# Gate and up products of a feed-forward as three products of rounded parts, with the low-rank product on 96 rows

## The reference

```python
mod = MOD_SCALE * jnp.tanh(attn @ A)
h = _rmsnorm(residual, ln2_w)
gate_pre = h @ W_in_base.T + mod * (h @ A) @ B
gate = jax.nn.silu(gate_pre)
up = h @ W_up_base.T
mlp_out = gate * up @ W_down.T
```

## Time and profile before

| | us |
|---|---|
| median of 3 runs | 1212.7 |
| lowest and highest | 1212.69, 1216.48 |
| the profiled execution | 1211.12 |
| its span, first to last instruction | 1209.3 |
| PE busy | 1038.0 (86%), x6621 |
| VectorE busy | 722.9 (60%), x1630 |
| ScalarE busy | 523.0 (43%), x881 |
| POOL busy | 308.2 (25%), x618 |
| mean granted TensorE clock | 0.917 of full |
| share of PE in the chain that ended last | 74% (VectorE 17%, ScalarE 4%) |
| page's slice from 393 to 423 us (14 of 40) | PE busy 7 tenths, clock 7 tenths of full |

### The profile page before, as it was taken

How to read it: one execution, slowest core, us unless ns; L and a number is a source line. 1 busy time by engine, 2 the same in 40 slices (tenths; PEclk the granted TensorE clock), 3 DMA queues, 4 the chain that set the end, 5 groups by cost and what they waited for, 6 DMA issues and landing times.

```text
span 1209.3 us, 18846 instructions
## 1 busy us (share of the span) xinstructions
PE 1038.0 (86%) x6621; PEld 660.5 (55%) x6621; DVE 722.9 (60%) x1630; ACT 523.0 (43%) x881; POOL 308.2 (25%) x618
## 2 busy tenths in 40 slices
PE   6399999999999788887889899962566978999997
PEld 4378888888887333333556337342223434556575
DVE  6965544544447568767655124487796665684744
ACT  3332222222243676665545411334553644544643
POOL 3024343434435555335331200010312200000000
PEclk9589999999999789899999999995767889999999
DMA  5202111121450000000000300020000000000000
GB/s 147 54 14 51 41 45 46 41 50 39 121 161 1 1 3 3 2 2 3 2 3 4 122 1 1 0 53 0 1 2 1 3 2 1 1 10 1 9 9 10
DMA packets 62461, 32.10 MB, mean 27 GB/s; under 512 B 47121, under 2 KB 61089, under 8 KB 62129
## 3 DMA queue, kind: packets, MB, share of 16 engines
q1 hardware_dynamic: 62384, 31.10, 9.6%
HBM read 29.64 MB, written 1.05 MB: 25 GB/s over the span
## 4 chain that ended last, share of the span: by engine, by line
PE 74%; DVE 17%; ACT 4%; issue 3%; POOL 1%; DMA 1%; POOLq 0%; DVEq 0%; SPq 0%; ACTq 0%; PEldq 0%
PE bank L780 16%; PE bank L806 8%; PE bank L915 4%; PE bank L1204 3%; PE bank L1388 3%; PE bank L1030 2%; PE bank L1133 2%; PE bank L998 2%; PE bank L1405 2%; PE bank L1390 2%; PE bank L960 2%; DVE mx L2379 2%; PE bank L1184 2%; PE bank L1220 1%; PE bank L1392 1%
## 5 line engine op out<-in xcount | busy, mean ns | idle before, releaser
L2379 DVE TENSOR_REDUCE mx<-bank 128x2 f32<-128x512 f32 (+1 forms) x176 | 117.7, 689 | 74.9 <-PE bank L1133 37.9
L1799 ACT ACTIVATE prob<-bank 128x512 f32<-128x512 f32 x176 | 103.2, 599 | 84.3 <-PE bank L1184 56.2
L1567 ACT ACTIVATE hhi<-hh 128x512 fp32r<-128x512 f32 x72 | 45.6, 633 | 156.1 <-DVE hh L2215 143.0
L2211 DVE TENSOR_TENSOR hu<-bank,sg 128x512 f32<-128x512 f32 x64 | 44.3, 692 | 92.1 <-PE bank L780 92.1
L780 PE MATMUL bank<-xh,wh 128*128 128x512 f32 x288 | 91.8, 400 | 0.3 <-DVE hh L2215 0.3
L780 PE MATMUL bank<-xh,wl 128*128 128x512 f32 x288 | 90.9, 396 | 0.0
L780 PE MATMUL bank<-xlo,wh 128*128 128x512 f32 x288 | 90.6, 396 | 0.0
L2203 DVE TENSOR_TENSOR hlo<-hh,hhi 128x512 fp32r<-128x512 f32 x72 | 57.2, 794 | 50.4 <-ACT hhi L1567 50.4
L2802 POOL TENSOR_TENSOR wl<-wraw,wh 128x512 fp32r<-128x512 f32 x72 | 81.6, 1133 | 13.0 <-POOL wh L2799 13.0
L1645 ACT ACTIVATE sg<-bank 128x512 f32<-128x512 f32 x72 | 43.1, 598 | 64.0 <-PE bank L780 64.0
L2799 POOL CAST wh<-wraw 128x512 fp32r<-128x512 f32 x72 | 37.1, 515 | 102.6 <-issue 51.8
(11 more groups left out here) (466 smaller groups left out, 2223.0 us busy)
## 6 DMA issues: line engine op xcount, KB each, us to landing
wraw<-in_L_ffn_wg_dram SPq DMA_DIRECT2D x64, 64.0 KB, 2.2
wraw<-in_L_ffn_wu_dram SPq DMA_DIRECT2D x64, 64.0 KB, 2.4
wraw<-in_L_ffn_wd_dram SPq DMA_DIRECT2D x32, 128.0 KB, 2.5
l_raw<-in_L_ffn_w_dram SPq DMA_DIRECT2D x2, 1024.0 KB, 6.6
mun<-in_L_ffn_mu_dram SPq DMA_DIRECT2D x1, 2048.0 KB, 7.5
xs<-in_x_dram SPq DMA_DIRECT2D x2, 512.0 KB, 4.5
w1s<-in_L_ffn_W_dram SPq DMA_DIRECT2D x2, 512.0 KB, 8.1
stage<-in_L_ffn_W_in_base_dram SPq DMA_DIRECT2D x1, 1024.0 KB, 8.1
```

The source lines that it names most:

```text
L1567: return act.activation(dst, src, ACT.Copy, scale=scale)
L1799: act.activation(t.prob[k][:, :], bank[3 + n % 2][:, :], ACT.Exp).then_inc(S("probs"), 1)
L2211: tt(hu[k % 2][:, :], bank[4 + (n + 1) % 4][:, :], sg[k % 2][:, :], ALU.mult).then_inc(once("up_used"), 1)
L2379: V.reduce_max(out_, bank[n % 3][:, :].rearrange("p (h t) -> p h t", h=heads), AX, negate=True)\
```

## The change

Weights, inputs and the low-rank factors of the feed-forward are taken apart into a part rounded to fp32r ("high") and the rest ("low"), and each product of gate and up becomes high x high + low x high + high x low. `am`, `bm`, `wa` and `mh` get three strips of 32 rows or columns, of which the first 16 hold data; in the low-rank product the strips of B are high, high, low and those of `mh` high, low, high, so that one matmul on 96 rows makes the sum of the three. POOL rounds `winT`, `wupT` and `bm` at the end of the first attention stream; VectorE makes the low parts after the meeting; ScalarE rounds `hT` between its tanh and sigmoid work; VectorE makes `hT_low`. New tiles lie over tiles that are no longer used; `gu` keeps 9 blocks instead of 16.

```diff
-        wa = sb("wa", [P, DC, R])
-        am = sb("am", [P, DC, R])
-        bm = sb("bm", [R, F1])
+        wa = sb("wa", [P, DC, 3 * 32])
+        am = sb("am", [P, DC, 3 * 32])
+        bm = sb("bm", [3 * 32, F1])
...
-            W(am[:, :, :], I["L1_ffn_A"].rearrange("(c p) r -> p c r", p=P)).then_inc(rest, 16)
-            W(bm[:, :], I["L1_ffn_B"]).then_inc(rest, 16)
+            sp.wait_ge(once("strips_cleared"), 1)
+            for j in range(3):
+                W(am[:, :, 32 * j:32 * j + R], I["L1_ffn_A"].rearrange("(c p) r -> p c r", p=P)).then_inc(rest, 16)
+                W(bm[32 * j:32 * j + R, :], I["L1_ffn_B"]).then_inc(rest, 16)
...
-                    mm(bank[4 + h][0:R, :], am[:, cc, :], hT[:, cc, h * 512:(h + 1) * 512], start=cc == 0, stop=cc == 1)
+                    mm(bank[4 + h][0:96, :], am[:, cc, :], hT[:, cc, h * 512:(h + 1) * 512], start=cc == 0, stop=cc == 1)
...
+                if n == 0:
+                    pe.wait_ge(once("ffn_weights_rounded"), 2)
+                    pe.wait_ge(once("ffn_weights_rest"), 2)
+                if f == 0:
+                    pe.wait_ge(once("hT_rounded"), h + 1)
                 g, u = bank[2 * (n % 2)], bank[2 * (n % 2) + 1]
-                for cc in range(DC):
-                    mm(g[:, :], winT[:, cc, fs], hT[:, cc, tok], start=cc == 0, stop=False)
-                for cc in range(DC):
-                    mm(u[:, :], wupT[:, cc, fs], hT[:, cc, tok], start=cc == 0, stop=cc == 1)
+                for to, high, low in ((g, win_high, win_low), (u, wup_high, wup_low)):
+                    for j, w in enumerate((high, low, high)):
+                        if f == 0 and j == 2:
+                            pe.wait_ge(once("hT_rest"), h + 1)
+                        for cc in range(DC):
+                            x = hT_low[:, cc, tok] if j == 2 else hT_high[:, h, cc, :]
+                            mm(to[:, :], w[:, cc, fs], x, start=j == 0 and cc == 0, stop=to is u and j == 2 and cc == 1)
                 pe.wait_ge(S("mh"), h + 1)
-                mm(g[:, :], bm[:, fs], mh[:, tok], start=False, stop=True).then_inc(S("ffn_up"), 1)
+                if n == 0:
+                    pe.wait_ge(once("bm_split"), 1)
+                mm(g[:, :], bm_parts[:, fs], mh[:, tok], start=False, stop=True).then_inc(S("ffn_up"), 1)
...
-                act.activation(modT[:, h * 512:(h + 1) * 512], bank[6 + h][0:R, :], ACT.Tanh).then_inc(S("modT"), 1)
+                act.activation(modT[:, h * 512:(h + 1) * 512], bank[6 + h][0:96, :], ACT.Tanh).then_inc(S("modT"), 1)
+
+            def round_inputs(h):
+
+                act.wait_ge(S("mod_ps"), HALVES)
+                copy(hT_high[:, h, :, :], hT[:, :, h * 512:(h + 1) * 512]).then_inc(once("hT_rounded"), 1)
+
+            round_inputs(0)
             for h in range(HALVES):
                 act.wait_ge(S("c_turned"), h + 1)
                 copy(cT8[:, h * 512:(h + 1) * 512], bank[6 + h][0:CD, :]).then_inc(S("cT2"), 1)
+            round_inputs(1)
...
             dve.wait_ge(once("batch_cleared"), 2)
 
+            for n, (low, whole, high) in enumerate(((win_low, winT, win_high), (wup_low, wupT, wup_high))):
+                dve.wait_ge(once("ffn_weights_rounded"), n + 1)
+                tt(low[:, :, :], whole[:, :, :], high[:, :, :].bitcast(F32), ALU.subtract).then_inc(once("ffn_weights_rest"), 1)
+            dve.wait_ge(once("bm_rounded"), 1)
+            tt(bm_parts[64:96, :], bm[64:96, :], bm_parts[64:96, :].bitcast(F32), ALU.subtract).then_inc(once("bm_split"), 1)
...
-                stt(out=mh[:, tok], in0=modT[:, tok], scalar=0.1, in1=bank[4 + h][0:R, :], op0=ALU.mult, op1=ALU.mult)\
-                    .then_inc(S("mh"), 1)
+                step(stt(out=modT[:, tok], in0=modT[:, tok], scalar=0.1, in1=bank[4 + h][0:96, :], op0=ALU.mult, op1=ALU.mult))
+                step(V.tensor_copy(mh[:, tok], modT[:, tok]))
+                tt(mh[32:64, tok], modT[32:64, tok], mh[32:64, tok].bitcast(F32), ALU.subtract).then_inc(S("mh"), 1)
+                dve.wait_ge(once("hT_rounded"), h + 1)
+                tt(hT_low[:, :, tok], hT[:, :, tok], hT_high[:, h, :, :].bitcast(F32), ALU.subtract).then_inc(once("hT_rest"), 1)
...
+            step(G.memset(am[:, :, :], 0.0), G.memset(bm[:, :], 0.0))
+            pool.sem_inc(once("strips_cleared"), 1)
             pool.sem_inc(once("picks"), 2)
...
             attention(step, "A")
+            pool.wait_ge(S("scores"), tiles_before("A", None))
+            pool.sem_inc(once("went_on"), 1)
+            for high, whole in ((win_high, winT), (wup_high, wupT)):
+                G.tensor_copy(high[:, :, :], whole[:, :, :]).then_inc(once("ffn_weights_rounded"), 1)
+            G.tensor_copy(bm_parts[:, :], bm[:, :]).then_inc(once("bm_rounded"), 1)
             end_loop(3 + 4)
```

More of the change, by code:

```diff
@@ L249, in flamingo @@
         early = top[0]
+        at_winT = top[0]
         winT = sb("winT", [P, DC, F1])
@@ L350, in flamingo @@
         after_operands = top[0]
+        at_hT = top[0]
         hT = sb("hT", [P, DC, TOKENS])
@@ L405, in flamingo @@
         top[0] = after_hT
-        gu = sb("gu", [P, HALVES, F1 // P, 512])
+        win_high = sb("win_high", [P, DC, F1], FR)
+        gu = sb("gu", [P, F1 // P + 1, 512])
         sgf = [sb(f"sgf{k}", [P, 512]) for k in range(2)]
-        modT = sb("modT", [R, TOKENS])
-        mh = sb("mh", [R, TOKENS])
+        wup_high = sb("wup_high", [P, DC, F1], FR)
+        modT = sb("modT", [3 * 32, TOKENS])
+        mh = sb("mh", [3 * 32, TOKENS], FR)
         assert top[0] <= after_c
+        top[0] = at_winT
+        win_low = sb("win_low", [P, DC, F1], FR)
+        wup_low = sb("wup_low", [P, DC, F1], FR)
+        top[0] = at_wqkvT
+        bm_parts = sb("bm_parts", [3 * 32, F1], FR)
+        top[0] = at_hT
+        hT_low = sb("hT_low", [P, DC, TOKENS], FR)
         top[0] = after_c
@@ L432, in flamingo @@
         mu2 = sb("mu2", [P, DC, SLOTS])
+        at_atT = top[0]
         atT = sb("atT", [P, DC, TOKENS])
+        top[0] = at_atT
+        hT_high = sb("hT_high", [P, HALVES, DC, 512], FR)
         top[0] = after_c
@@ L525, in prep_bank @@
             return ((6, 7, 3) if g < 12 else (4, 5, 3))[g % 3]
-        REST = len(rowsD) - 2 + 8
+        REST = len(rowsD) - 2 + 12
         def clear(eng, spared=()):
@@ L872, in _ @@
                 for cc in range(DC):
-                    last = mm(bank[7][:, m * R:(m + 1) * R], wo[:, cc, m * P:(m + 1) * P], am[:, cc, :],
+                    last = mm(bank[7][:, m * 96:(m + 1) * 96], wo[:, cc, m * P:(m + 1) * P], am[:, cc, :],
                               start=cc == 0, stop=cc == DC - 1)
@@ L1367, in _ @@
                 for cc in range(DC):
-                    last = mm(bank[6 + h][0:R, :], wa[:, cc, :], atT[:, cc, h * 512:(h + 1) * 512], start=cc == 0, stop=cc == 1)
+                    last = mm(bank[6 + h][0:96, :], wa[:, cc, :], atT[:, cc, h * 512:(h + 1) * 512], start=cc == 0, stop=cc == 1)
                 last.then_inc(S("mod_ps"), 1)
@@ L1385, in gate_and_up, with hidden_of @@
                     pe.wait_ge(S("ffn_gu"), n - 1)
-                g, u = bank[2 * (n % 2)], bank[2 * (n % 2) + 1]
-                for cc in range(DC):
-                    mm(g[:, :], winT[:, cc, fs], hT[:, cc, tok], start=cc == 0, stop=False)
-                for cc in range(DC):
-                    mm(u[:, :], wupT[:, cc, fs], hT[:, cc, tok], start=cc == 0, stop=cc == 1)
-                pe.wait_ge(S("mh"), h + 1)
-                mm(g[:, :], bm[:, fs], mh[:, tok], start=False, stop=True).then_inc(S("ffn_up"), 1)
+                if n == 0:
[3 more added lines that the diff above has]
+                    pe.wait_ge(once("hT_rounded"), h + 1)
+                g, u = bank[2 * (n % 2)], bank[2 * (n % 2) + 1]
+                for to, high, low in ((g, win_high, win_low), (u, wup_high, wup_low)):
[5 more added lines that the diff above has]
+                            mm(to[:, :], w[:, cc, fs], x, start=j == 0 and cc == 0, stop=to is u and j == 2 and cc == 1)
+                pe.wait_ge(S("mh"), h + 1)
+                if n == 0:
+                    pe.wait_ge(once("bm_split"), 1)
+                mm(g[:, :], bm_parts[:, fs], mh[:, tok], start=False, stop=True).then_inc(S("ffn_up"), 1)
+            def hidden_of(h, f):
+                return gu[:, f if h == 0 or f > 0 else F1 // P, :]
             def down(h, i):
@@ L1404, in down @@
                     pe.wait_ge(S("ffn_gu"), 8 * h + f + 1)
-                    last = mm(bank[(4, 0)[h] + n % 2][:, 0:D], gu[:, h, f, i * P:(i + 1) * P], wdT[:, f, :],
+                    last = mm(bank[(4, 0)[h] + n % 2][:, 0:D], hidden_of(h, f)[:, i * P:(i + 1) * P], wdT[:, f, :],
                               start=f == 0, stop=f == F1 // P - 1)
@@ L1680, in _ @@
             act.wait_ge(once("wa_made"), 1)
-            copy(wa[:, :, :], bank[7][:, 0:DC * R].rearrange("p (m r) -> p m r", m=DC)).then_inc(once("prepared"), 1)
```

(3 more changed lines are left out.)

## The result

| | before | after |
|---|---|---|
| median, us | 1212.7 (12 runs, 1208.02 to 1218.09) | 1201.74 (12 runs, 1197.71 to 1209.37) |
| ratio, 95% interval | | 0.9917 (0.990 to 0.9935) |
| the profiled execution, us | 1211.12 | 1200.49 |
| its span, us | 1209.3 | 1198.7 |
| mean granted TensorE clock | 0.917 | 0.913 |

What follows compares the result with a forecast made beforehand. TensorE was taken as the bound, carrying 74% of the chain and all of layer 1's gated feed-forward. 15.0 + 7.7 - 9.2 - 2.0 = 11.5 us saved gave 1201.2 us by the median, range 1192 to 1208.

Steps and rivals of the forecast that it cites:

- the clock of the second `sj` product: PE's product before the first block, after its pause: taken at some 0.95 us, with no low-clock loss counted.
- A block of 3.0 us, no switch with 96 rows: Gate and up on PE: a block costs 3.01 us instead of 4.68, with no row-count switch.
- the other bound: Low-rank product in the 16 blocks: a row-count switch of 0.2 us each, 3 us in all.
- Nine blocks, 15.0 us: First nine blocks on PE: 1.67 us saved in each, 15.0 us by the first half's down products.
- Opening of the batch, +1.0: POOL's casts ahead of the batch: it opens 1.0 us later, at 674.5, with bounds of -1.0 to +1.4.
- The lock: Head: POOL's squaring of `mun` holds VectorE's second subtraction until 683.8; first block 9.2 us late instead of 3.7.
- Second half, 7.7 us: From D, the end of the first down products, to the last block's end: 41.3 us instead of 49.0.
- The range of its own bounds: Whole kernel: 1198 to 1206 us, from bounds on batch opening, lock order, second-half clock loss and row-count switch.
- no meeting on the port: Rival, head: VectorE and POOL run side by side, or squaring ends first; 19.0 us saved, 1193.7; chance 0.14.
- The clock does not come back: Rival, first nine blocks: all at 1.2 GHz, 6.02 us each; 1226; chance 0.03.
- the fp32r product streams slower here: Rival, blocks: fp32r matmuls slower than in the expert stage; at 0.30 us each 1211.4, no gain; chance 0.05.
- The longer head: Rival: slow casts, low clock through two blocks and behind both second-half waits; 6.8 us more, 1208.1; chance 0.10.

Runs made afterwards that it cites:

- e3: Changed kernel with the low-rank product left as before, plain f32 on 16 rows, without the third subtraction; 1216.49 us, ratio 1.0008 to the kernel before.
- e2: Changed kernel with nine extra matmuls filling PE's pause before the `sj` products, their results overwritten; 1200.83 us, ratio 0.991 to the kernel before.
- e4: Changed kernel with only the stacked 96-row low-rank product kept; gate and up plain f32 as before; 1200.99 us, ratio 0.9895 to the kernel before.
- e7: Changed kernel with POOL's square of `mun` after both `hT_low` halves and `slot_norms` before second-half block 2 on VectorE; 1197.49 us in one run.
- e1: Changed kernel with POOL's square of `mun` waiting until both halves of `hT_low` are made; 1196.07 us, ratio 0.9854 to the kernel before.
- e5: Changed kernel with the square of `mun` late, `slot_norms` earlier, and `mh` of both halves ahead of `hT_low`; 1194.77 us, ratio 0.9839 to before.
- e6: Changed kernel with POOL's square of `mun` made in eight pieces, each waited for; 1200.41 us in one run.
- e8: The kernel before, profiled again with no edit; 1210.27 us in one run.

## Why the prediction was right

The forecast was 1201.2 us and its sum 11.5 us saved; the medians differ by 11.0 and the profiles by 10.6. The mechanism was right in the main. Two steps were off, the victim of the lock and the clock of the second `sj` product. That the sum came within 1 us is luck in part, since the errors below have both signs and one kernel's runs spread over 12 us. The terms, one by one:

- **A block of 3.0 us, no switch with 96 rows.** 2.99. The rows of the expert stage carried over to other operands as they were. e3 shows the switch and its size; the other bound (3 us in all) falls.
- **Nine blocks, 15.0 us.** 9 x (4.68 - 2.99) = 15.2, of which 2.0 went to the low clock as forecast (first block 5.0 us instead of 3.0; e2 shows the cause by taking it away).
- **Opening of the batch, +1.0.** Measured +0.1 (1.81 us behind VectorE's end instead of 1.69). This term was too large. The casts took what the slope gave, 1.89, 1.84 and 1.04 us, their sum near the lower bound. They are on the chain, but the last one with 0.14 us only: POOL's semaphore instructions (POOLq, 669.79 to 671.10 in the chain above) run beside the rest of it, so that the batch opens 0.1 us later, by SP's load, than before. Of the bounds given, "not later at all if the semaphore instructions run ahead of the casts" was the right end. e4, which has only the cast of B, opens at the same 5.4 us: the two large casts put nothing in front.
- **The lock.** Right in kind and in size, wrong in whom it caught. The prediction set POOL's request 1.3 us behind the start of VectorE's first subtraction and had the second one held. It came during the second and held the third (7.92 us). e7, with neither the lock nor the low clock in the head, gives the head without it: 2.5 us longer than before, where the prediction had 2.7. e3 and e4 show that the victim is whoever comes next. The copy in `mh`, which no row before showed and which was put at 0.35 to 0.7 us, took 0.43. From the opening to the first block 8.2 us more were forecast and 9.4 measured; 1.0 of the difference is the second `sj` product at the low clock, 2.04 us instead of 1.05, which the prediction left at full speed although it had the clock low from the pause on. That is a step that it missed, next to one that it had. It was made up for by the opening, so that the two together gave 9.5 where 9.2 stood.
- **Second half, 7.7 us.** From D to the end of the last block 42.4 us instead of 41.3, that is 6.7 saved. Both waits of PE came, ahead of `turn_inputs` and of `turn_slot_parts`, in the order and for the reasons given, 1.6 and 1.1 us long where 1.8 and 1.4 were forecast. What was mis-sized is the low clock: `slot_products` took 11.1 us instead of 10.16 and the block behind it 5.5 instead of 4.9. Over the ten profiles `slot_products` takes 8.6 to 11.1 us, by when the clock falls in it; the prediction carried the 10.16 of one execution over to a kernel whose work ahead of it is another.

The range of its own bounds, 1198 to 1206, is not their sum, which reaches from 1199.1 to 1208.9; no working is given for it.

Among the rivals, "no meeting on the port" is refuted by the rows of 7.92, 7.04 and 7.03 us, and its price by e1 and e7. "The clock does not come back" is refuted by the second block, at 3.0 us. That the fp32r product streams slower here is refuted by the block. The longer head did not come: the casts took 1.9 us each, only the first block ran at the low clock, and behind both new waits of the second half the blocks took 3.0 us again. The low clock in the transposes of e1 and e5 is a cost that no rival names, and the profile of the change doesn't have it.

The Trainium skill (SBUF — State Buffer, "Who interferes with whom") says that VectorE and GpSimd share a pair of ports as an exclusive lock, and that a VectorE instruction with two SBUF inputs contends for it with a GpSimd instruction that reads SBUF. The trace agrees, with 6.7 and 6.8 us of waiting where the prediction had a case of 1.07 us.

What stays open is why the transposes get the full clock in eight of the ten profiles and half of it in e1 and e5. PE's idle before them is the same 2.65 us in after, e7, e1 and e5; in e1 the granted clock falls at 668.8, 1.5 us ahead of them, in after and e7 it doesn't fall. Equally open is what sets the moment at which it falls in `slot_products`. No run here tells these apart.

## What to carry to other kernels

Splitting f32 products into rounded ones pays on TensorE by the streamed time (0.86 us for a plain product of 512 columns, 0.69 for its three), but its casts and subtractions need room on VectorE and GpSimd in front of the first product. Look up what the other engine does in that window: a long two-input instruction of GpSimd held a short one of VectorE on the chain for nearly its full length, and moving it behind the window takes one line and gave 3 to 7 us of the head here. Price the parts of such a change apart: here the low-rank product, whose row count differed from its neighbours', gave by itself as much as the whole change with a quarter of the added casts and subtractions (3.4 us of VectorE and 1.0 of POOL, of 17.3 us with ScalarE's). A term measured in one execution at a changing clock deserves a range.

## What the runs showed of the hardware

- The waiting engine gets its turn when the running instruction ends, even if the holder has more in its queue (e6: POOL after every second of VectorE's dot products, which have no gap between them); and the profile counts the wait as part of the waiting instruction (8.94 us for a square that takes 7.02 alone, 7.04 for a dot product that takes 0.22).
- A 16-row f32 product of 512 columns between 128-row products costs 1.3 us, a 96-row fp32r one 0.24 (e3 against after). Of the 1.3, 0.86 is what a 128-row f32 product takes, 0.19 more lies in the product's own row and 0.24 in the products behind.
- The 64 small products of `slot_products` take 8.6 to 11.1 us, and the length follows the granted clock: it falls 5.4 us after their start in the shortest case and 2.6 in the longest.
- Two executions of one kernel differ by 2.5 us in where a stage starts and by 1.7 in what follows it (e8), while every stretch within the stage repeats to 0.1. A single profile can't tell such a difference from the effect of an edit.
